# Replicated-row fetches for a selective scan: partitions ordered by channel, then state

## The reference

```python
dt = softplus(einsum('btr,dr->btd', dt_low, W_dt) + b_dt)
A = -exp(A_log)                                      # (256 channels, 16 states)
dA = exp(dt[..., None] * A)
dBx = dt[..., None] * B_ssm[:, :, None, :] * x_conv[..., None]
_, h = associative_scan(comb, (dA, dBx), axis=1)     # over time
y = einsum('btdn,btn->btd', h, C_ssm)
y = y * silu(z) + D_param * x_conv
```

## Time and profile before

| | |
|---|---|
| median of 3 runs | 2933.4 us (2932.14 to 2947.86) |
| profiled execution | 2938.84 us, its span 2937.0 us |
| mean granted TensorE clock | 0.926 of full speed |
| instructions | 37,056 |
| busy: PE, DVE, ACT, POOL | 2427.5, 1902.7, 1633.0, 1814.4 us |
| the chain that ended last | PE 39%, DVE 20%, issue 15%, POOL 12%, ACT 7%, DMA 6% |

### The profile page before, as it was taken

How to read it: one execution, slowest core, us unless ns; L and a number is a source line. 1 busy time by engine, 2 the same in 40 slices (tenths; PEclk the granted TensorE clock), 3 DMA queues, 4 the chain that set the end, 5 groups by cost and what they waited for, 6 DMA issues and landing times.

```text
span 2937.0 us, 37056 instructions
## 1 busy us (share of the span) xinstructions
PE 2427.5 (83%) x9792; PEld 1229.2 (42%) x9792; DVE 1902.7 (65%) x3116; ACT 1633.0 (56%) x4152; POOL 1814.4 (62%) x2311
## 2 busy tenths in 40 slices
PE   5789988989898898989898988989898988767422
PEld 3555544444444444444444444444444444312100
DVE  2445567676767767676767677676767677565533
ACT  3654656666566656666666656666565656423322
POOL 1012267575757668585858677585857667676865
PEclk9989999999999999999999999999999999978555
DMA  6424455555656655555656555655556564434241
GB/s 131 52 45 62 77 113 110 115 109 112 118 112 118 107 118 109 126 100 107 121 119 116 103 117 104 133 99 120 106 120 116 101 115 86 116 86 115 72 104 41
DMA packets 495419, 304.94 MB, mean 104 GB/s; under 512 B 347257, under 2 KB 413737, under 8 KB 494761
## 3 DMA queue, kind: packets, MB, share of 16 engines
q1 hardware_dynamic: 495212, 302.58, 52.1%
HBM read 242.21 MB, written 26.74 MB: 92 GB/s over the span
## 4 chain that ended last, share of the span: by engine, by line
PE 39%; DVE 20%; issue 15%; POOL 12%; ACT 7%; DMA 6%; SPq 1%; DVEq 0%; POOLq 0%; ACTq 0%
PE bank L511 7%; PE bank L820 6%; DMA work<-dt_rows 5%; PE bank L802 5%; POOL work L1073 4%; DVE work L1066 4%; POOL work L1060 3%; DVE zh L816 3%; PE bank L1085 3%; PE bank L538 2%; PE bank L938 2%; DVE step L912 2%; PE bank L838 2%; DVE nmax L518 2%; ACT th L809 2%
## 5 line engine op out<-in xcount | busy, mean ns | idle before, releaser
L1060 POOL TENSOR_TENSOR work<-work,bc 128x512 f32<-128x512 f32 x512 | 653.2, 1281 | 249.2 <-DMA work<-dt_rows 128.0
L1066 DVE TENSOR_TENSOR_SCAN work<-bank,work 128x512 f32<-128x512 f32 x512 | 622.0, 1215 | 216.6 <-POOL work L1060 164.9
L1073 POOL TENSOR_TENSOR work<-work,bc 128x512 f32<-128x512 f32 x512 | 658.3, 1291 | 111.8 <-DVE work L1066 110.1
L833 POOL TENSOR_TENSOR zh<-zh,w_bc 128x512 f32<-128x512 f32 x256 | 325.2, 1270 | 485.1 <-DVE zh L826 485.1
L1049 ACT ACTIVATE bank<-work,neg_a 128x510 f32<-128x510 f32 x512 | 353.0, 689 | 466.1 <-DVE work L1066 368.9
L528 ACT ACTIVATE probs<-bank,nmax 128x256 f32<-128x256 f32 x1024 | 474.9, 471 | 213.8 <-DVE nmax L518 210.8
L511 PE MATMUL bank<-ke,q_all 96*128 96x256 f32 x2048 | 561.0, 398 | 11.7 <-DMA q_all<-q_rows 11.7
L511 PEld LDWEIGHTS bank<-ke,q_all 96*128 96x128 f32 x2048 | 384.4, 197 | 218.6 <-issue 152.4
L518 DVE TENSOR_REDUCE nmax<-bank 128x2 f32<-128x512 f32 x512 | 347.7, 679 | 162.3 <-PE bank L511 152.7
L820 PE MATMUL bank<-h_b,w_t 128*128 128x512 f32 x512 | 295.8, 661 | 131.8 <-DVE zh L816 123.6
L538 PEld LDWEIGHTS bank<-ident,probs 128*128 128x128 f32 x2048 | 257.3, 146 | 286.0 <-issue 207.6
(11 more groups left out here) (190 smaller groups left out, 2508.0 us busy)
## 6 DMA issues: line engine op xcount, KB each, us to landing
work<-dt_rows SPq DMA_DIRECT2D x256, 512.0 KB
w_bc<-w_rows_d SPq DMA_DIRECT2D x256, 256.0 KB, 9.2
ke<-ke SPq DMA_DIRECT2D x128, 256.0 KB, 8.5
bc<-bc_rows SPq DMA_DIRECT2D x64, 256.0 KB
x_in<-in_x SPq DMA_DIRECT2D x32, 256.0 KB, 6.7
q_all<-q_rows SPq DMA_DIRECT2D x512, 8.0 KB
dt_rows<-step SPq DMA_DIRECT2D x16, 512.0 KB, 2.9
dt_rows<-step SPq DMA_DIRECT2D x32, 256.0 KB, 2.3
```

What stands on the lines that cost most here:

```text
L833: nc.gpsimd.tensor_tensor(zh[:, n % 3, :], zh[:, n % 3, :], w_bc[:, n % WB, :], ALU.mult).then_inc(m_p, 1)
L1060: nc.gpsimd.tensor_tensor(hb[at % HB], ring[n % RING][:, 1, :], bc[:, s, :], ALU.mult).then_inc(s_dbx, 1)
L1066: nc.vector.tensor_tensor_scan(hb[at % HB], bank[6][:, :], hb[at % HB], 0.0, ALU.mult, ALU.add).then_inc(s_h, 1)
L1073: nc.gpsimd.tensor_tensor(hb[at % HB], hb[at % HB], bc[:, SG + batch(m)[2], :], ALU.mult).then_inc(s_hc, 1)
```

## The change

The partitions of a batch are ordered by channel, then state: partition 8 c + s. Each source pattern that repeats rows gets its dimensions in the other order: the `bc` fetch from (8 rows, 16 copies) to (16 copies, 8 rows), the `dt_rows` fetch from (8 copies, 16 rows) to (16 rows, 8 copies). `sel_d` and `a_log` are laid out to match.

```diff
@@ s_rows_in_sync
-            sp.dma_start(bc[:, k, :], bc_rows[8 * k:8 * k + 8, :].unsqueeze(1).broadcast_to([8, DC, TOK])).then_inc(bc_in[k], 16)
+            sp.dma_start(bc[:, k, :], bc_rows[8 * k:8 * k + 8, :].unsqueeze(0).broadcast_to([DC, P // DC, TOK])).then_inc(bc_in[k], 16)
@@ s_fetch_sync
             sp.dma_start(ring[n % RING].rearrange("p r t -> p (r t)"),
-                         dt_rows[DC * j:DC * (j + 1), :].unsqueeze(0).broadcast_to([P // DC, DC, 2 * TOK])).then_inc(s_in[n % RING], 16)
+                         dt_rows[DC * j:DC * (j + 1), :].unsqueeze(1).broadcast_to([DC, P // DC, 2 * TOK])).then_inc(s_in[n % RING], 16)
@@ kernel
-    sel_d = (ah[:, None, None] % DC + DC * np.arange(2)[None, :, None] == np.arange(32)[None, None, :]).astype(one)
+    sel_d = (ah[:, None, None] // (P // DC) + DC * np.arange(2)[None, :, None] == np.arange(32)[None, None, :]).astype(one)
@@
-        "a_log": f["L1_attn_A_log"].reshape(FETCHES, DC, SG, P // DC).transpose(3, 1, 0, 2),
+        "a_log": f["L1_attn_A_log"].reshape(FETCHES, DC, SG, P // DC).transpose(1, 3, 0, 2),
```

## The result

The changed kernel takes 2863.3 us (median of 4 runs, 2857.8 to 2869.6) against 2938.7 us for the kernel before on the same chip: a ratio of 0.974, 95% interval 0.970 to 0.978. That is 75 us or 2.6%, where 52 were forecast. The profiled execution took 2863.71 us, its span is 2861.9.

The account below looks back on a forecast made before the run. TensorE sets the pace, held up through other engines by broadcast fetches that fill eight of 16 DMA engines. Middle 30, head 3 and tail 19 make 52 us off a median of 2933.4: 2881 us, range 2828 to 2924.

Parts of the forecast that it names:

- The half that hides a full resource: Stretches of broadcast fetches alone: a DMA share stuck at 0.52 to 0.54 means eight engines full and eight idle.
- The packet time: `dt_rows` fetch: sixteen engines at the same packet time, so 4.0 us become 2.0 us.
- The middle, 30 us by 2.5 a pair: Twelve middle pairs: less TensorE idling, mainly before L538, taken at 2.5 us a pair, 30 us.
- The head, 3 us: First scan: its waits shrink by one pair's worth, 3 us.
- The tail, 19 us: After 2,580 us: 13 us from `dt_rows` waits, 5 before the first `bc` batch, 1 for the pair before; 19 us.
- `bc` covered in the middle: Middle pairs: GpSimd's 41.4 us of waits for `bc` are covered by VectorE's and TensorE's own order.
- Other transfers at nothing: `w_bc`, `ke` and `x_in` find engines 8 to 15 busier; priced at nothing, as the low eight stay the busier.
- Rival D: Slower: sixteen engines move no more bytes than eight, rate under about 150 GB/s, `w_bc` queues behind; 2952 us, chance 0.06.
- E: Share in stretches of `dt_rows` alone stays at 0.52 since another dimension chooses the engines; 2933 us, chance 0.05.
- B: Middle: the removed wait turns up before the next matmul, only half the tail comes; 12 us, 2921, chance 0.09.
- A: The forecast itself, whole kernel: 2881 us, bounds 19 to 95 us of gain (2914 to 2838), chance 0.66.
- C: More than the sum: GpSimd and ScalarE run ahead at more places, 6 us a pair; 108 us, 2825, chance 0.14.

Follow-up runs that it names:

- two_halves: Changed kernel, new order kept, each `dt_rows` fetch cut into two DMAs of 8 rows by 8 copies, first dimension 8: 2881.7 us, ratio 0.980.
- middle_pairs: Changed kernel with the new patterns only in the second to the fourteenth pair, old ones elsewhere: 2893.3 us, ratio 0.987 to the kernel before.
- first_pair: Changed kernel with the new patterns only in the first pair's fetches, old ones elsewhere: 2920.0 us, ratio 0.996 to the kernel before.
- last_pairs: Changed kernel with the new patterns only in the last two pairs, old ones elsewhere: 2915.1 us, ratio 0.995 to the kernel before.
- dt_alone: Changed kernel with the `bc` fetch given its old pattern back, `dt_rows` keeping the new one: 2866.5 us, ratio 0.975 to the kernel before.
- dt_16copies_8rows: Changed kernel, but each `dt_rows` fetch takes 16 copies of a block of 8 rows, first dimension 16: 2865.3 us, ratio 0.975.
- bc_alone: Changed kernel with the `dt_rows` fetch given its old pattern back, `bc` keeping the new one: 2922.2 us, ratio 0.997 to the kernel before.
- fetch_later: Changed kernel with the `dt_rows` fetches due 4 steps later, behind the B and C rows: 2882.7 us, ratio 0.981 to the kernel before.
- dt_8rows_16copies: Changed kernel, but each `dt_rows` fetch takes 8 rows, each 16 times, first dimension 8: 2910.3 us, ratio 0.990 to the kernel before.
- two_halves_together: Changed kernel, each `dt_rows` fetch cut into two DMAs of 8 copies by 8 rows, engines reading the same rows together: 2920.4 us, ratio 0.993.

## Why the prediction was right, and where its sizes were off

**The half that hides a full resource: right.** The stretches of the earlier trace rows with a share stuck at 0.5 were the key. Across first dimensions of 4, 8 and 16 the share followed, and the same mean share (52%) hid both a kernel that waits for DMA and one that doesn't.

**The packet time "at each engine's old pace": right in size, wrong as a rule.** The changed fetch lasts 2.0 us as taken. Yet the pace is not a constant: 24 GB/s per engine with four engines, 15 to 16 with eight that go through the same rows, 18 to 24 with eight that repeat rows of their own (`two_halves`), 16 with sixteen.

**The middle, 30 us by 2.5 a pair: 40 by the profiles, 38 by `middle_pairs`.** The priced part, idling of TensorE, is 25.7 us or 2.1 a pair, and 18.7 of it went at the very place that the sum was built on, before L538, where 28.1 had stood. This step holds. The term that was mis-sized is the clock: nothing in the sum, 5 us in the widest case. The two profiles put 14.4 us there, but `first_pair` has the changed kernel's busy time with the old patterns, so how much of the 14.4 is the change's stays open. What is firm is the whole: some 75 us gained in two sessions (ratios 0.974 and 0.975), and 45 us of less idling in the profiles; the rest, some 30, is that the same matmuls were busy for less time, 2,397.9 us for 2,427.5.

**The head, 3 us: 11 by `first_pair`, 11.7 by the section.** It is the term that was most wrong, by a factor of four. 4.0 us are less idling and 7.7 a clock of 1.00 for 0.95. Here the clock goes with the pattern somewhat better than in the middle: busy 149.5 to 149.8 us in the kernel before, `last_pairs` and `middle_pairs`, 142.0 to 143.3 in the changed kernel (twice), `dt_alone` and `dt_16copies_8rows`, but 146.6 in `first_pair` itself and 145.9 in `bc_alone`, which has the old pattern. I had treated the first scan as one more pair of the middle, though the waits for `dt_rows` before 537 us, 18.1 of GpSimd's 128.0, were over twice the 7.8 us of a pair of the middle.

**The tail, 19 us: 16 by the section, 15 by `last_pairs`.** The store reached its fetch 2.5 us sooner and the wait shrank by 4.7, where 5 was told. The prediction worked out 12 us for the tail from the fixed 2 us of the Trainium skill. That step was unsound: a fixed part makes the saving a smaller share of a fetch, but the 2 us saved on each stay 2 us. The measured 15 says nothing for or against the rule. All 16.6 us of `dt_rows` waits went; if the 5 hold, about 10 of them showed in the time, where 13 were told.

**`bc` covered in the middle: it fits.** `bc_alone` can't show it, since 35.4 us of the waits are left in its middle, where the earlier trace rows has 41.4. `two_halves` can: it keeps most of the waits in the middle for both fetches,

```profile
POOL work L1061 <- DMA work<-dt_rows: 41.4, 29, 2.4
POOL work L1061 <- DMA bc<-bc_rows: 31.4, 12, 3.2
```

and TensorE idles 194.8 us there, 5.1 more than in the changed kernel. So the 31.4 us for `bc` cost at most 5 us of idling; what waits cost through the clock, as in `fetch_later`, isn't in that number.

**Other transfers at nothing: no cost shows.** `w_bc`, which shares the upper engines now, lands in 5.0 us at the median where it took 9.2. That follows the `dt_rows` pattern: 9.2 in `bc_alone`, 5.0 in `dt_alone`. Rival D's condition, under 150 GB/s, wasn't met.

**The rivals.** E is out by the share, D by the rate, B by the idling that went. The result lies between A (52) and C (108); C's mechanism, GpSimd and ScalarE ahead at more places, isn't what made the difference to 52: TensorE's idling shrank by no more than the sum had, and what came on top is busy time. So the 45 us of less idling answer to the 52 forecast; the other 30 came from a part that was put at nothing, and the total stayed in the range with them because the range was wide.

## What to carry to other kernels

When a mean DMA share looks harmless, look at stretches of one transfer alone: a share stuck at 1/2 or 1/4 under a backlog says that the pattern runs on 8 or 4 of 16 engines, and the order of its dimensions is the cure. Where such a pattern can't have 16, let each engine repeat a row of its own rather than have all of them walk the same rows. And read a gain from two profiles in two parts, idle and busy time of TensorE: here the idle part of the middle followed the patterns, while the busy part moved by 14 us without them.

## What the runs showed of the hardware that was not expected

- Eight engines that went through the same 4 KB rows of DRAM together moved 117 to 127 GB/s; eight that read rows of their own moved 143 to 193, into the same partitions with DMAs of the same size. With one DMA over 128 partitions (`dt_8rows_16copies`) the gap was much smaller in such stretches, 135 against 131, though the program gained 21 us; why is open, and the partitions that one engine writes were not separated from the size of the DMA.
- `two_halves_together` gained 20 us and `bc_alone` 8, with the same `bc` and both with eight engines that go through the same rows; why the cut into two DMAs helps is open.
- Four engines reached 98 GB/s, three quarters of what eight did in the kernel before, though they too went through the same rows together.
- The gain doesn't follow GpSimd's waits in proportion: 128 us of them to 54 (`two_halves`) brought 2.0%, 54 to none the last 0.6; with 89.6 us `fetch_later` was as fast as `two_halves`.
- The interval between the first two pairs takes 115.7 or 121.6 us with the same program text up to there, by a granted clock of 0.96 or 0.90. One profile against another can be off by that much, and the middle by 14 us.
- TensorE's time can be lost without its idling: `fetch_later` idles it as long in the middle as the changed kernel does and takes 17.5 us more over the same 7,255 matmuls.
